# Two key chunks of each second query tile in one DRAM round trip, dense weights laid out by the host: fp32 attention layer with a cluster-gated dense layer

## The reference, cut to what matters

```python
h = layernorm(x)
qkv = h @ w_qkv                      # 512 x 6144: 32 query heads, 8 key/value heads, head size 128
scores = q @ k^T * 128**-0.5 + bias  # causal; bias = -slope[h] * sqrt(distance)
x = x + (softmax(scores) @ v) @ w_o  # w_o: 4096 x 512

h = layernorm(x)
dots = softmax(h @ centroids.T / 0.1)        # 64 clusters
hits = dots > 0.01
dense = h @ weight.T + bias                  # weight: 512 x 512
x = x + where(query_sel & row_sel[assignments], dense, 0)
```

## Time and profile before

| | |
|---|---|
| median of the runs | 1240.78 us |
| the profiled execution, its own time | 1241.91 us |
| span of its records | 1240.3 us |
| PE busy | 1225.9 us, 99% |
| PE's granted clock | 0.999 of full speed |
| DVE, ACT, POOL busy | 57%, 60%, 47% |
| DMA engines | 41.3% for the SP queue's kind, 3.4% for POOL's |
| one unit in the loop | about 35.6 us |

### The profile page before, as it was taken

How to read it: one execution, slowest core, us unless ns; L and a number is a source line. 1 busy time by engine, 2 the same in 40 slices (tenths; PEclk the granted TensorE clock), 3 DMA queues, 4 the chain that set the end, 5 groups by cost and what they waited for, 6 DMA issues and landing times.

```text
span 1240.3 us, 20680 instructions
## 1 busy us (share of the span) xinstructions
PE 1225.9 (99%) x5880; PEld 1028.8 (83%) x5880; DVE 711.5 (57%) x1638; ACT 747.9 (60%) x2169; POOL 578.6 (47%) x512
## 2 busy tenths in 40 slices
PE   8999999999999999999999999999999999999998
PEld 7788888888888888888888888888888888888877
DVE  7676554545555555555555555555545555567677
ACT  4876556566655565666556656665566666556543
POOL 3533546336452646326463555436463364334323
PEclk9999999999999999999999999999999999999999
DMA  6553545445454445444443554535454454523303
GB/s 204 174 166 111 164 141 169 144 135 176 138 169 133 143 155 168 152 136 151 154 163 116 165 165 152 165 114 169 138 166 146 140 171 147 183 85 117 96 10 136
DMA packets 209563, 180.72 MB, mean 146 GB/s; under 512 B 12096, under 2 KB 162368, under 8 KB 209536
## 3 DMA queue, kind: packets, MB, share of 16 engines
q1 hardware_dynamic: 205504, 167.55, 41.3%
q0 software_dynamic: 4032, 12.85, 3.4%
HBM read 101.45 MB, written 78.91 MB: 145 GB/s over the span
## 4 chain that ended last, share of the span: by engine, by line
PE 93%; DVE 2%; POOL 1%; issue 1%; ACT 1%; SPq 1%; DMA 0%; POOLq 0%; DVEq 0%; ACTq 0%
PE ps L1560 91%; PE ps L1585 1%; POOL ring L650 1%; DMA acc<-in_L_attn_w_qkv 0%; POOL wo_lo L609 0%; PE ps L1595 0%; ACT prob L864 0%; PE ps L1689 0%; DVE stats L1067 0%; POOL vT L658 0%; DVE prob L1116 0%; DVE acc L1185 0%; PE ps L1700 0%; POOL wo_hi L607 0%; DVE xnT L1121 0%
## 5 line engine op out<-in xcount | busy, mean ns | idle before, releaser
L1560 PE MATMUL ps<-xnT,wqkv_hi 128*128 (+2 forms) x1560 | 479.8, 389 | 0.1
L650 POOL TENSOR_TENSOR ring<-ring_whole,pT_hi 128x512 fp32r<-128x512 f32 x189 | 244.5, 1294 | 380.2 <-ACT pT_hi L842 376.2
L1560 PEld LDWEIGHTS ps<-xnT,wqkv_hi 128*128 128x128 f32 x1560 | 290.0, 188 | 58.3 <-issue 0.5
L1560 PE MATMUL ps<-xnT,wqkv_lo 128*128 (+1 forms) x780 | 302.7, 388 | 0.0
L851 ACT ACTIVATE prob<-prob,negmax 128x256 f32<-128x256 f32 (+1 forms) x384 | 176.7, 462 | 151.5 <-DVE negmax L1208 120.0
L1560 PE MATMUL ps<-wo_hi,oT_hi 128*128 128x512 f32 x512 | 200.3, 391 | 1.1 <-DVE oT_lo L1179 0.8
L1560 PE MATMUL ps<-wo_lo,oT_hi 128*128 128x512 f32 x512 | 199.6, 390 | 0.0
L1560 PE MATMUL ps<-wo_hi,oT_lo 128*128 128x512 f32 x512 | 199.3, 389 | 0.0
L842 ACT ACTIVATE pT_hi<-ring_whole 128x512 fp32r<-128x512 f32 x189 | 117.9, 624 | 123.4 <-DMA ring_whole<-turned 83.5
L1185 DVE TENSOR_TENSOR acc<-ps,acc 128x512 f32 (+1 forms) x128 | 88.4, 690 | 154.9 <-PE ps L1560 154.9
L864 ACT ACTIVATE prob<-prob,rinv 128x256 f32<-128x256 f32 (+1 forms) x384 | 150.1, 463 | 38.2 <-DVE rinv L1214 38.2
(11 more groups left out here) (159 smaller groups left out, 1740.2 us busy)
## 6 DMA issues: line engine op xcount, KB each, us to landing
turned<-ring_whole SPq DMA_DIRECT2D x189, 256.0 KB, 2.1
ring_whole<-turned SPq DMA_DIRECT2D x189, 256.0 KB, 2.9
turned_v<-vT SPq DMA_DIRECT2D x32, 256.0 KB, 2.0
turned_s<-prob SPq DMA_DIRECT2D x32, 256.0 KB, 2.1
prob<-turned_s SPq DMA_DIRECT2D x32, 256.0 KB, 2.8
turned_s<-vT SPq DMA_DIRECT2D x32, 256.0 KB, 2.0
vT<-turned_s SPq DMA_DIRECT2D x32, 256.0 KB, 3.8
vT<-turned_v SPq DMA_DIRECT2D x31, 256.0 KB, 2.7
```

Of the source, the lines that this page charges most:

```text
L650: pool.tensor_tensor(ring_slot(c), whole_slot(c), pT_hi[:, c % 2, :].bitcast(F32), ALU.subtract).then_inc(pT_lo_done, 1)
L1560: ins = pe.matmul(dst, l, r, start=start and m == 0, stop=stop and m == n - 1)
```

## The change

Its parts:

1. Chunks 0 and 1, and chunks 3 and 4, go out in one transfer of 512 KB and come back in one (`turn_pair_out`, `turn_pair_in`), in all 32 units but for chunks 3 and 4 of the last. The write waits for the second of the two; ACT waits for the pair before either chunk. Chunks 2 and 5 travel alone as before.
2. The host gives the dense weight and the centroids transposed. PE's 20 transposes and the splits of ACT and DVE behind them go; POOL splits the weights from SBUF instead (`split_dense`, ten operations) ahead of unit 30.
3. In units 2, 30 and 31 the layernorm's statistics come earlier on DVE, its square root earlier on ACT, three of its transposes come after the fifth projection and the fourth after `apply_v(3)`, and PE waits for fewer low parts ahead of the next scores.
4. In unit 1 the fourth early layernorm tile is transposed later, and `apply_v(1)` runs inside the sixth projection.
5. POOL makes the high part of the fourth `w_o` slice ahead of the low part of chunk 3, no longer behind it.
6. In the tail, chunk 2's high part comes ahead of the last exponentials, POOL's low part of it ahead of one bias step, and some DVE and PE steps swap.

```diff
+            def turn_pair_out(v, c):
+
+                sp.wait_ge(p_turned, v * CHUNKS + c + 2)
+                sp.dma_start(turned[c:c + 2].rearrange("a p x -> p a x"), ring_whole[:, c:c + 2, :]).then_inc(p_out[c], 16)
+
+            def turn_pair_in(v, c):
+
+                sp.wait_ge(p_out[c], v * 16 + 16)
+                sp.dma_start(ring_whole[:, c:c + 2, :].rearrange("p a (i x) -> p (a i) x", i=P // BLK),
+                             turned[c:c + 2].rearrange("a (i r) (j x) -> (r j) (a i) x", i=P // BLK, j=P // BLK)).then_inc(p_in[c], 16)
...
             def turn_second(v):
-                turn_out(v, 3)
-                turn_out(v, 4)
-                turn_in(v, 3)
-                turn_in(v, 4)
+                turn_pair_out(v, 3)
+                turn_pair_in(v, 3)
                 turn_out(v, 5)
                 turn_in(v, 5)
...
-                for h in range(1, HPG):
-                    pT_lo_part(u + 1, h)
-                    split_o(g, h)
-                    if h == 1:
-                        load_after(g, NC + 1)
+                pT_lo_part(u + 1, 1)
+                split_o(g, 1)
+                load_after(g, NC + 1)
+                pT_lo_part(u + 1, 2)
+                split_o(g, 2)
+                split_o(g, 3, 0)
+                pT_lo_part(u + 1, 3)
+                split_o(g, 3, 1)
...
+                if last:
+                    for c in range(NC + 1):
+                        split_dense(c)
                 plain_body(u + 2)
...
             pT_lo_part(UNITS, 1)
             sum_scores(UNITS - 1, 1)
+            pT_lo_part(UNITS, 2)
             with_bias(1, 2)
-            pT_lo_part(UNITS, 2)
             with_bias(1, 3)
...
-                    act.wait_ge(p_in[c], u * 16)
+                    act.wait_ge(p_in[3 * (c // 3) + 2 * (c % 3 == 2)], u * 16)
...
                     if L is not None and attn:
-                        pe.wait_ge(ln_lo_done, L * TPQ + TPQ)
+                        pe.wait_ge(ln_lo_done, L * TPQ + 2)
                     scores_by_key(u, 0)
...
+                if L is not None and attn:
+                    pe.wait_ge(ln_lo_done, L * TPQ + 3)
...
-                project(u, 5)
+                project(u, 5, (0, 1, 2))
                 apply_v(u, 1)
+                project(u, 5, (3,))
                 apply_v(u, 2)
+                ln_transpose(2, 3)
...
-            for t in range(NC):
-                for c in range(NC):
-                    ins = pe.transpose(ps[:, WT_BANKS[t], c * P:(c + 1) * P], w_raw[:, t, c * P:(c + 1) * P], ident[:])
-                ins.then_inc(wT_mm, 1)
```

More of the change, by code:

```diff
@@ L567, in _ @@
             scores_out(last, 1)
[L568 to L571, removed]
+            turn_pair_out(last, 0)
+            turn_pair_in(last, 0)
             turn_out(last, 2)
@@ L638, in split_qkv, with split_o @@
                     split(raw[:, c % 2, :], wqkv_hi[:, c, :], wqkv_lo[:, c, :], g * (2 * NC) + SETUP + c + 1)
-            def split_o(g, h):
-                if isinstance(g, int) and g == 0:
+            def split_o(g, h, part=None):
+                if part == 1:
+                    pass
+                elif isinstance(g, int) and g == 0:
                     pool.wait_ge(first_o_loaded[h % 2], 16 * (h // 2 + 1))
@@ L644, in split_o @@
                     pool.wait_ge(raw_loaded[h % 2], g * 64 - 32 + 16 * (h // 2 + 1))
-                split(raw[:, h % 2, 0:HID], wo_hi[:, h, :], wo_lo[:, h, :], g * (2 * NC) + SETUP + NC + h + 1)
+                if part != 1:
+                    split_hi(raw[:, h % 2, 0:HID], wo_hi[:, h, :])
+                if part != 0:
+                    split_lo(raw[:, h % 2, 0:HID], wo_hi[:, h, :], wo_lo[:, h, :], g * (2 * NC) + SETUP + NC + h + 1)
             def pT_lo_part(u, c):
@@ L1279, in body @@
                     if attn and i == 0:
+                        if L is not None:
+                            if p is not None:
+                                dve.wait_ge(added, u * QTILES)
+                            ln_stats_of(L, source, 0)
+                            ln_stats_of(L, source, 1)
                         invert_sums(u - 1, 2)
+                        if L is not None:
+                            ln_stats_of(L, source, 2)
+                            ln_stats_of(L, source, 3)
                     if attn and i == 1:
                         find_max(u - 1, 1)
+                        if L is not None:
+                            ln_var(L)
                     if proj and i < PROJ_OUTS - 1:
@@ L1346, in body @@
                     return
+                if L is not None:
+                    ln_lo(L, 3, quad)
                 add_out(u, 0)
-                if L is not None:
-                    for j in ln_tiles_at(u, PROJ_OUTS):
-                        ln_lo(L, j, quad)
                 turn_scores(u, 0)
@@ L1611, in project_first, with project @@
                     ins.then_inc(qkv_mm, 1)
-            def project(u, i):
+            def project(u, i, chunks=range(NC)):
                 col = HPG * D if i == 0 else (HPG + 1) * D if i == PROJ_OUTS - 1 else (i - 1) * D
@@ L1618, in project @@
                           (flat[:, bass.ds(at[c], UT)], flat[:, bass.ds(at[NC + c], UT)])) for c in range(NC)]
-                for c in range(NC):
+                for c in chunks:
                     if i == 0:
@@ L1622, in project @@
                     ins = three_pass(ps[:, proj_bank(u, i), :], terms[c:c + 1], c == 0, c == NC - 1)
-                ins.then_inc(qkv_mm, 1)
+                if NC - 1 in chunks:
+                    ins.then_inc(qkv_mm, 1)
             def transpose_probs(u, c):
@@ L1756, in body @@
                             apply_v(u, i - lag)
-                    if L is not None and PROJ_OUTS > i >= 4:
+                    if L is not None:
                         if attn and i == 4:
@@ L1768, in body @@
                     project_out(u, 0)
-                    if L is not None:
-                        for j in ln_tiles_at(u, PROJ_OUTS):
-                            ln_transpose(L, j)
                     apply_v(u, CHUNKS - 2)
```

142 lines of the change are left out of this document (71 added, 71 removed).

## The result

The changed kernel takes 1321.57 us (median of four runs, 1318.13 to 1323.11), the kernel before 1240.74 us beside it: ratio 1.0646, 95% interval 1.0633 to 1.0659. The forecast was 1257.4 us with a range to 1272. The direction was right, the loss of 81 us is five times the forecast one. The profiled execution took 1323.11 us with a span of 1321.2 us; PE's mean granted clock was 0.990, against 0.999 before.

What follows compares the result with a forecast made beforehand. PE, busy 99% of the span, was taken to bound the kernel. New waits of 22.8 us (3.9 + 7.0 + 11.9) less 6.2 us gained gave +16.6 us, so 1257.4 us, 1.3% slower, range 1238 to 1272 us.

Steps and rivals of the forecast that it cites:

- Third and fourth units: Units of a group, 13 in the loop: PE waits 0.3 us each at chunk 3, 3.9 us in all.
- Read of 512 KB: Return leg of chunks 3 and 4: one transfer takes 3.6 us, 0.7 more than the first read alone; bounds 3.3 to 4.1.
- The pair of chunks 0 and 1: Lands 1.9 us later while ACT is busy with exponentials: cost 0, or up to 0.6 us in units beside a load.
- The start and the write: Outgoing leg of chunks 3 and 4: issued 0.6 us later, then 2.7 us for 512 KB, 0.6 us more.
- Second units: Second unit of a group, tighter slack: PE waits 0.9 to 1.0 us, bounds 0.4 and 1.6; seven units, 7.0 us.
- First units: First unit of a group: PE waits 1.7 us because the pair's read meets weight loads; seven units, 11.9 us.
- The collision with the `w_o` loads: In a group's first unit, POOL's two 256 KB loads hold the pair's read up for about 1.6 us.
- The rate taken from one window of 0.6 us: Where both queues had work, POOL's moved 0.20 MB and SP's 0.05 MB; used for the loads beside the pair's read.
- What the other parts give: Gain from removed transposes, layernorm waits, unit 1 and the tail: 6.2 us, bounds 4.4 and 6.7.
- That cover is partly spent: Ahead of unit 30, POOL's ten new operations (8.6 us) fit its 12.5 us idle; up to 1 us delay, cost 0.
- The page's rule on merging: Skill's advice to coalesce small transfers: each pair would come out no later, sum -6.2 us instead of +16.6.
- Much slower: Rival: second 256 KB of the read costs its full 1.3 us, first pair late too; about 1273 us, chance 0.05 beyond 1272.

Runs made afterwards that it cites:

- the singles: The changed kernel with all pair transfers put back as two of 256 KB each way, all else staying changed: 1235.9 us, ratio to before 0.9959.

## Why the prediction was off

**What bounds it, and where it would hurt: right.** PE's chain in one piece, the slack of 1.7 us at chunk 3, the DMA as the late part, the waits released by POOL's ring in every unit of the loop: all of it is in the profile after, and undoing the pairs takes all of the loss away.

**Third and fourth units, 0.3 us forecast, 1.9 measured (mean).** Two steps failed. "Read of 512 KB: ... As one transfer I take those 3.6 us": it took 4.4 at the median of both pairs, and 4.7 for chunks 3 and 4, the only pair of the kernel with the second pair alone; both are outside the bound of 4.1. Most of that is the read itself: held free of its neighbour it still took 4.1 to 4.5 us to ACT (5.0 in unit 1), so even the bound was hardly enough. The rest is the queue: SP issues chunk 5's write 0.5 us behind the read now, where before it went out 1.4 us after the first of two. The other step is "The pair of chunks 0 and 1 ... Cost 0". The text saw that if it is late, chunk 3 is late with it by up to 0.6 us; that is what happens, but in every unit, not only beside a load. In unit 18, then, 0.6 (first pair) + 0.6 (start) + 0.7 (write) + 1.6 (read) = 3.5 us stands against 1.7. The start and the write were priced well (0.6 and 0.6).

**Second units, 1.0 us forecast, 2.2 + 0.26 measured.** The same two steps, with less slack to begin with. The `wo_lo` behind the ring is a wait of its own and small, as the change's new order had it.

**First units, 1.7 us forecast, 2.0 measured: about the right size for the wrong reason.** The collision with the `w_o` loads was to hold the read up by 1.6 us. With the second pair alone, first units wait 1.32 us and third ones 1.21; with merged reads 0.80 and 0.76. So the loads cost 0.1 us there, and the sum of the first units came out near by luck. The rate taken from one window of 0.6 us did not carry over. And "Before, chunk 3's read had landed by then" was not so:

```profile
731.75 1.04 SPq L449 DMA_DIRECT2D ring_whole<-turned  x2
```

Issued at 731.75, it landed 2.8 us later, at 734.6, with POOL's loads issued at 733.48 in flight beside it. It took no longer than elsewhere, so the trace of before already spoke against the collision. What took longer beside the loads was chunk 5's write: issued at 733.19, landed 4.6 us later.

**The waits, summed.** 22.8 us were forecast, POOL's ring and `wo_ready` together show 60.2.

**TensorE's clock: missing altogether.** No term allowed for what a wait does to the matmuls behind it: 12.3 us of lower clock and about 11 us of pipeline.

**What the other parts give, 6.2 us forecast: about right**, 5.2 by the singles beside their own runs of before (1241.1 - 1235.9). The 20 transposes are gone, and so are the three waits of 0.76 us. "That cover is partly spent ... 0" was wrong for the dense splits: POOL is ready 1.5 us after PE needs it in the singles, 2.0 us in the changed kernel.

**The page's rule on merging** would have put the result at 6 us faster. It doesn't hold here, as the working said. The Trainium skill has the opposite one too ("Perfetto Trace Analysis", DMA Optimizations): splitting a DMA may let the task end sooner where the DMA engines are generally idle. They are 42% busy in the changed kernel, and the kernel with single transfers is 86 us faster.

**The rivals.** "Much slower" had the right mechanism: the second 256 KB at its full price and the first pair late too. It was given 0.05 beyond 1272 us, and its own numbers stopped at 1.3 us for the second 256 KB (measured 1.6 in unit 18, some 0.4 of it by the write behind). A chain whose forecast delay of 1.9 us sits 0.2 us above its slack turns each further 0.1 us into 2.7 us over 27 units. So the range had to be wide on the slow side, several times the 15 us it gave, for two unpriced neighbours (the write behind, the other pair ahead) alone.

## What to carry to other kernels

Where a consumer takes two transfers one after the other, merging them makes the first as late as the second, on both legs of a round trip. Add up all the delays of one chain, those of earlier merges included, before comparing them with its slack, because past the slack every tenth of a microsecond counts once per unit. Price a longer transfer with whatever its queue issues behind it in flight, and price a wait of PE at more than its length. Keep the change without the pairs: at 1235.9 us that version is faster than both kernels.

## What the runs showed that was not expected

- PE's granted clock fell to 0.50 in 8 of the changed kernel's 27 loop units, behind waits of 1.8 to 3.0 us; others of 1.6 to 2.4 us had no such effect. With the second pair alone it fell four times, once as a wait of 0.26 us began, 0.9 us of work after one of 1.61 us, and once behind waits of 1.0 and 1.5 us with 1 us of work between; with merged writes it fell four times as well. Behind the 31 waits of up to 1.05 us of the kernel with merged reads it never fell. What decides it between 1.6 and 2.4 us was not settled.
- A DRAM-to-SBUF read in pieces of 512 bytes of the scores grew from 3.0 to 4.3 us (issue to ACT) for twice the bytes, an SBUF-to-DRAM write in rows of 2 KB per partition from 2.1 to 2.8.
- A 256 KB write issued 0.5 us behind a 512 KB read landed after 4.7 us in unit 18, where behind two reads of 256 KB it had taken 2.9 and, held until the pair's read had landed, took 2.0; it made the read 0.4 us longer.
- The kernel before has only 0.8 us of slack at chunk 5 in first units (median), less than chunk 3's 1.7: two of the experiments lose time there, by chunk 5's write beside the `w_o` loads or behind two reads.
- Eight thrown-away matmuls ahead of a wait of some 2 us made the kernel 12.7 us faster.
